# POOL takes over the layer norm of the third and fourth tile of each graph in a graph-attention kernel on one core

## What is computed

```python
def _layernorm(x, axis=-1, eps=1e-05):
    m = jnp.mean(x, axis=axis, keepdims=True)
    v = jnp.var(x, axis=axis, keepdims=True)
    return (x - m) / jnp.sqrt(v + eps)
...
    a = jnp.einsum('bhnd,bhmd->bhnm', q, k) * scale + bias      # bias = adj + adj
    p = jax.nn.softmax(a, axis=-1)
    o = jnp.einsum('bhnm,bhmd->bhnd', p, v)
...
x = _layernorm(x + attention(x, adj) , axis=-1)                 # this one is touched
x = _layernorm(x + experts(x, adj), axis=-1)
```

## Time and profile before

| | us |
|---|---|
| median of 3 runs | 2458.79 (2457.8 to 2460.12) |
| profiled execution | 2458.45 |
| its span on the core | 2456.7 |
| PE busy | 2212.4 (90%) |
| POOL busy | 1746.4 (71%) |
| DVE busy | 1708.7 (70%) |
| ACT busy | 1597.5 (65%) |

### The profile page before, as it was taken

The page is one execution under the profiler, slowest core; times in us unless marked ns, Lnnn a source line. Parts: engine busy times, 40 slices in busy tenths (PEclk is TensorE's granted clock), DMA queues, the critical chain, the costliest instruction groups (busy, mean ns, idle before and its releaser), DMA issues.

```text
span 2456.7 us, 48589 instructions
## 1 busy us (share of the span) xinstructions
PE 2212.4 (90%) x14496; PEld 1706.3 (69%) x14496; DVE 1708.7 (70%) x4350; ACT 1597.5 (65%) x3792; POOL 1746.4 (71%) x3196
## 2 busy tenths in 40 slices
PE   3678999999999999999999999999999999998764
PEld 2456677777777777677767777677777777676653
DVE  2476776768586776768586776768686776767568
ACT  0456766666666766667676766667676766666457
POOL 0578877777787877777687777777787777777224
PEclk7789999999999999999999999999999999999987
DMA  6488465565747556565747556574747566474877
GB/s 222 127 276 261 127 196 183 174 196 147 232 128 249 147 176 193 172 191 142 244 135 235 154 182 189 155 214 138 251 127 217 164 191 190 149 221 128 316 269 288
DMA packets 213188, 472.65 MB, mean 192 GB/s; under 512 B 40832, under 2 KB 49024, under 8 KB 206144
## 3 DMA queue, kind: packets, MB, share of 16 engines
q1 hardware_dynamic: 212928, 469.55, 61.9%
HBM read 270.16 MB, written 65.01 MB: 136 GB/s over the span
## 4 chain that ended last, share of the span: by engine, by line
PE 73%; DVE 12%; issue 5%; SPq 3%; POOL 3%; ACT 3%; DMA 1%; DVEq 0%; POOLq 0%; ACTq 0%
PE t_bank L379 15%; PE p_bank L283 13%; PE p_bank L284 13%; PE p_bank L285 13%; PE o_bank L398 9%; PE s_bank L362 8%; SPq L765 2%; DVE att L547 2%; POOL fold L734 1%; DVE x L601 1%; DVE xt L601 1%; PE o_bank L389 1%; POOL fold L736 1%; ACT att L455 1%; ACT pt L519 1%
## 5 line engine op out<-in xcount | busy, mean ns | idle before, releaser
L734 POOL TENSOR_TENSOR fold<-att 128x256 f32<-128x256 f32 x1024 | 774.9, 757 | 430.4 <-DVE nmax L547 337.1
L547 DVE CUSTOM_DVE_ANT_0 att<-s_bank,adj_t 128x512 f32<-128x512 f32 x1024 | 694.3, 682 | 378.0 <-PE s_bank L362 377.1
L455 ACT ACTIVATE att<-att,nmax 128x512 f32<-128x512 f32 x1024 | 738.4, 722 | 193.2 <-POOL fold L734 168.7
L519 ACT ACTIVATE pt<-t_bank 128x512 f32<-128x512 f32 x768 | 452.1, 596 | 410.7 <-PE o_bank L398 259.9
L379 PE MATMUL t_bank<-ident,att 128*128 128x128 f32 x4096 | 629.3, 277 | 13.4 <-ACT pt L519 6.9
L379 PEld LDWEIGHTS t_bank<-ident,att 128*128 128x128 f32 x4096 | 501.1, 142 | 195.9 <-issue 65.5
L362 PE MATMUL s_bank<-k_stack,q_stack 128*128 128x512 f32 x1024 | 498.3, 488 | 84.9 <-DVE nmax L547 84.5
L736 POOL TENSOR_TENSOR fold<-fold 128x128 f32<-128x128 f32 x1024 | 497.5, 486 | 80.3
L741 POOL TENSOR_TENSOR fold<-fold 128x64 f32<-128x64 f32 x1024 | 350.6, 342 | 80.2
L362 PEld LDWEIGHTS s_bank<-k_stack,q_stack 128*128 128x128 f32 x1024 | 198.1, 193 | 105.3 <-DVE nmax L547 104.2
L398 PE MATMUL o_bank<-pt,v 128*32 128x256 f32 x4096 | 250.1, 385 | 5.3 <-issue 4.3
(11 more groups left out here) (354 smaller groups left out, 3631.1 us busy)
## 6 DMA issues: line engine op xcount, KB each, us to landing
q_stack<-qk_t SPq DMA_DIRECT2D x1024, 64.0 KB, 3.2
k_stack<-qk_t SPq DMA_DIRECT2D x1024, 64.0 KB, 2.0
qk_w<-qk_split SPq DMA_DIRECT2D x123, 512.0 KB, 5.3
slot_a<-expert_split SPq DMA_DIRECT2D x16, 2048.0 KB, 8.1
slot_b<-vo_split SPq DMA_DIRECT2D x15, 2048.0 KB, 8.7
slot_a<-vo_split SPq DMA_DIRECT2D x15, 2048.0 KB, 9.4
stage<-in_xT SPq DMA_DIRECT2D x16, 1024.0 KB, 5.5
adj_t<-in_adj SPq DMA_DIRECT2D x64, 256.0 KB, 7.8
```

The lines of the kernel that those rows point to most:

```text
L455: eng.activation(att[:, u % 4, j, :], att[:, u % 4, j, :], ACT.Exp, bias=nmax[:, u % 4, j:j + 1], scale=-1.0, accum_out=rsum[:, u % 4, j:j ...
L519: eng.activation(pt[:, j, :, (u % 2) * P:(u % 2 + 1) * P], t_bank[r % 2][:, :].rearrange("p (m n) -> p m n", m=NT), ACT.Copy).then_inc(act ...
L547: eng.tensor_tensor_reduce(out=att[:, u % 4, j, :], in0=s_bank[r % 2][:, :], in1=adj_t[:, t, :], scale=-2.0, scalar=3.0e38, op0=ALU.add, o ...
L734: eng.tensor_tensor(fold1[:, :], a[:, 0:256], a[:, 256:512], ALU.add).then_inc(pool_fold1, 1)
```

## The change

POOL applies the norm to tiles 2 and 3, directly behind its folds in quarter (6, 3) and one wait for `dve_newton`. DVE keeps tiles 0 and 1 where they were, and its two instructions in quarter (7, 0) are gone. A new semaphore `pool_x1` counts POOL's tiles; ACT waits for it before it reads tile 2 or 3, and SP before the store.

```diff
@@ act_slot
-                        wait(eng, dve_x1, b, NT, t + 1 - NT)
+                        wait(eng, dve_x1 if t < 2 else pool_x1, b, 2, t % 2 + 1 - 2)
@@ dve_slot
-                if (u, j) in ((6, 3), (7, 0)) and has_prev:
-                    for t in (0, 1) if j == 3 else (2, 3):
+                if (u, j) == (6, 3) and has_prev:
+                    for t in (0, 1):
                         eng.tensor_scalar(x1_home(b)[:, t, :], x1_home(b)[:, t, :], ln_mv[:, t, 0:1], ln_rstd[:, t:t + 1],
                                           ALU.subtract, ALU.mult).then_inc(dve_x1, 1)
@@ pool_slot
                     eng.tensor_tensor(fold2[:, uu % 2, jj, :], fold1[:, 0:P // 2], fold1[:, P // 2:P],
                                       ALU.add).then_inc(pool_fold2, 1)
+                if (u, j) == (6, 3) and has_prev:
+                    wait(eng, dve_newton, b, 3, 0)
+                    for t in (2, 3):
+                        eng.tensor_scalar(x1_home(b)[:, t, :], x1_home(b)[:, t, :], ln_mv[:, t, 0:1],
+                                          ln_rstd[:, t:t + 1], ALU.subtract, ALU.mult).then_inc(pool_x1, 1)
@@ sp_slot
-                wait(eng, dve_x1, b, NT, 0)
+                wait(eng, dve_x1, b, 2, 0)
+                wait(eng, pool_x1, b, 2, 0)
```

More of the change, by code:

```diff
@@ L158, in build_gnn_layers @@
         pool_fold1 = sem("pool_fold1"); pool_halved = sem("pool_halved"); pool_fold2 = sem("pool_fold2"); pool_at = sem("pool_at")
-        pool_const = sem("pool_const")
+        pool_const = sem("pool_const"); pool_x1 = sem("pool_x1")
         ld_const = sem("ld_const"); ld_raw = sem("ld_raw"); st_split = sem("st_split")
```

## The result

The changed kernel takes 2502.44 us (median of 4 runs, 2501.91 to 2503.92); the one before took 2459.11 in the same series. The ratio is 1.0175, with a 95% interval from 1.0162 to 1.0188: slower by 43 us, where 2460.2 was forecast and the range ended at 2466.

The account below looks back on a forecast made before the run. PE, busy for 90%, was taken to bound the kernel, with DVE counting only where PE waits. 14 x (0.45 - 0.30) = +2.1, less 1.0, plus 0.3 made +1.4: median about 2460.2 us, range 2453.5 to 2466.

Parts of the forecast that it names:

- Where the removal counts: DVE's second norm pair is off the chain; removing it helps only through the copy that pv waits for, 0 to 0.30.
- the 0.30: Before pv: an earlier copy on DVE lets pv start 0.30 us earlier in each of fourteen graphs.
- the pause of 1.00 us: Last graph with attention: PE's wait for logits 41, behind the removed pair, goes; 1.0 us gained once.
- The price of a tile on POOL: POOL after quarter (6, 3): 0.77 plus 0.17 us for tile 2, 0.77 plus at most 0.27 for tile 3.
- My upper bound of 1.29: POOL's tiles: 1.29 us each, from a two-input operation of the same size, used in the POOL-late rival.
- POOL becomes late: Rival, chance 0.10: fold 40 starts after 1269.1 and its chain of 4.15 us delays pv by 0.7; 2468.0 us.
- the clock: Rival, chance 0.06: PE's clock falls to 1.2 GHz behind the longer pause for logits 40; +10 us, 2470.
- PE's pause for logits 40: Sign before the scores: PE's pause at 1.5 to 1.6 us instead of 1.12.
- The collision of 0.45 us: First norm pair: POOL's first tile falls on DVE's second instruction, delaying logits 40 and the scores by 0.45 us.
- the full lock: Rival, chance 0.12: DVE's second norm instruction waits for POOL's whole tile and ends 0.76 us later; 2464.6 us.
- The tail: The tail's norm meets the same collision once, at +0.4 us at most.
- Nothing on the chain waits for them: POOL's later folds and SP's store move by less than 1 us; nothing on the chain waits for them.

Follow-up runs that it names:

- e3_left_out: The changed kernel without POOL's two norm instructions and the waits for them, so tiles 2 and 3 miss the norm's last step: 2456.04 us.
- e4_one_tile: The changed kernel with tile 2 given back to DVE and only tile 3 on POOL, in the slow subtract form: 2454.28 us.
- e5_moved: e2_add with DVE's pair of tiles 0 and 1 moved from the end of quarter (6, 3) to quarter (7, 0), behind logits 40: 2448.10 us.
- e6_dummy: The kernel before, DVE norming all four tiles, plus two add-mult instructions on POOL in quarter (6, 3) whose result nobody uses: 2465.28 us.
- e7_task_first: The changed kernel, slow subtract form, with ACT's high part of the projection put ahead of exponential 40 in quarter (7, 2): 2492.16 us.
- e9_lag1: The kernel before plus one useless add-mult instruction of 128x512 on POOL, behind the fold in quarter (7, 3): 2450.05 us.
- e2_add: The changed kernel, but POOL first writes the negated means of tiles 2 and 3 and adds them in place of subtracting the means: 2447.33 us.

## Why the prediction was wrong, step by step

- *Where the removal counts* held. The second pair was off the chain, and taking it away gave 0.7 to 5.2 us (e3_left_out). Its size was too high: the 0.30 came in six graphs of fourteen. In the last graph with attention the pause of 1.00 us is gone in the changed kernel, as forecast, and pv starts 5.43 us after the pair instead of 6.35.
- *The price of a tile on POOL* is the step that failed. "I take 0.77 plus 0.17 ... for tile 2, and 0.77 plus at most 0.27 for tile 3" was measured as 4.60 us for the pair, so POOL was free for fold 40 after 4.57 us and not after 1.8 to 2.0. The nearest rows were of the same engine, operation name and size, but they were mult with add (L1045) and add with mult (L1053); the new instruction subtracts. My upper bound of 1.29 was a bound over sizes and inputs, and none over the arithmetic.
- *The rival "POOL becomes late"* was the true course, with its chain of 4.15 us and its threshold: with 4.57 us on POOL its own formula puts fold 40 at 1266.65 + 4.57 = 1271.22 and pv at 1275.37, 2.28 after 1273.09; the pause grew by 2.25. From the start of fold 40 to pv it is 4.15 or 4.16 us in thirteen of the fourteen graphs of the changed kernel, and 4.16 or 4.17 in twelve of those of e4_one_tile. It had a chance of 0.10 and a price of 2468, since the size fed to it was too small.
- *The rival "the clock"* came on top: a longer pause, and a fall to 1.2 GHz behind it in about half of the graphs, about 2 us each. I had hung it on the pause for logits 40 and weighed it alone, though both rivals lengthen a pause and go together.
- *PE's pause for logits 40*, forecast at 1.5 to 1.6 us, stayed at 1.11 and 1.13 in the two graphs of the changed kernel that have it. In the other twelve the clock had fallen ahead of the pair, and PE, at 1.2 GHz, has no pause there.
- *The collision of 0.45 us*, and the 0.76 of the full lock, did not come in this place: the pair kept its 1.08 in the changed kernel, and POOL's tile took 0.47 longer. At other distances it comes (e5_moved, e6_dummy, the tail). The price from the earlier trace rows was that of a start 0.06 us after the pair, and not of 0.33.
- *The tail* was priced at 0.4 us at most, for a collision, and cost 2.4, for POOL's two slow tiles.
- *"Nothing on the chain waits for them"*, of POOL's later folds, was wrong twice. DVE's sum in slot 8 had 1 us of room and waits once POOL is 2 us late (e7_task_first). And the distance of the folds to DVE's low parts in slot 8 is worth 0.8 us a graph (e9_lag1). In the changed kernel it returned a part: 859 against 926 ns in the mean of 60 low parts, 4 us.

Together for one graph in which the clock holds: 2.25 at pv, less 0.81 behind it (15.89 to 15.08), is the 1.4 between 139.2 and 140.6; where the clock falls, 2.0 to 2.2 more, all of it behind pv (17.06 to 17.30). What stays open is why it falls behind one pause of 2.48 us and not behind the next of the same length. The traces show only what came ahead: in the seven graphs where it holds, PE's clock had also fallen 2.1 to 3.2 us ahead of the norm's first pair; in the seven where it falls, it had fallen earlier than that (3.4 to 3.7 us, five graphs) or not at all (two).

## What to carry to other kernels

The price of an instruction on another engine must come from a row with the same arithmetic as well as the same size; where none exists, the bound has to be as wide as the doubt, and a kernel near a threshold needs that rival priced at the far end. An engine that runs without pauses passes lateness on to every consumer in turn, so cutting one link of the chain only finds the next. And when instructions of two engines lengthen each other in every round, the distance between them is a parameter of its own: it can be worth more than the work that is moved, in either direction, and it should be read before and after, in the single rounds too, for they may already differ.

## What the runs showed that I had not expected

- POOL's tensor-scalar on 128x512 f32 takes 0.76 to 1.05 us as add with mult or mult with add (up to 1.34 in single places, as in the tail of e2_add), and 2.07 to 2.55 with a subtract in either position. DVE's own takes 0.53 with subtract and mult.
- When a DVE instruction and a POOL instruction meet, who pays depends on fractions of a microsecond: a pair of two-input DVE instructions took 1.40, 1.62, 1.86 or 1.98 us as POOL's large fold started 1.00 after it, 1.21 after it, 0.33 after it, or 0.16 before it, and the collision can just as well fall on POOL's short fold (0.66 in place of 0.32).
- One useless instruction of 0.77 us in each graph made the kernel 0.4% faster.
